# One bank for each head of a maxima piece, filled and read in turns, in the third causal attention of a decoder kernel

## What is computed

```python
H = 16; HD = D // H; NR = 64
c_q = einsum('bhtd,ld->bhtl', xh, W_DQ)
q_c = einsum('bhtl,dl->bhtd', c_q, W_UQ)
q_c_norm = _rms_norm(q_c, q_norm_w)
q_r = einsum('bhtd,rd->bhtr', q_c_norm, W_QR)
q = concatenate([q_c_norm, q_r]);  k = concatenate([k_c_norm, k_r])
scores = einsum('bhqd,bhkd->bhqk', q, k) * scale
causal = triu(full((t, t), -inf), k=1)
attn = softmax(scores + causal, axis=-1)
ctx = einsum('bhqk,bhkd->bhqd', attn, v_c)
out = einsum('bhtd,od->bhto', ctx, W_O)
```

## Time and profile before

| what | us |
|---|---|
| median of three runs | 3476.15 (3475.05 to 3477.63) |
| the profiled execution's own time | 3473.25 |
| its span in the profile | 3471.5 |
| TensorE matmul busy | 3022.5 (87%) |
| VectorE busy | 1858.8 (54%) |
| ScalarE busy | 1336.8 (39%) |
| GpSimd busy | 1138.8 (33%) |
| reductions L3621 (192), busy / idle ahead of them | 182.3 / 107.6 |
| maxima matmuls L3511 (384), busy / idle ahead of them | 92.2 / 46.8 |
| first and last reduction L3621 start at | 2952.0, 3269.2 |

### The profile page before, as it was taken

One profiled execution on the slowest core, in us unless ns is written; L12 is line 12 of the kernel. 1 busy time (PEld: TensorE's weight loads), 2 busy tenths in 40 slices (PEclk: granted clock), 3 DMA queues, 4 the chain that ended last, 5 costly groups with the idle time before them and its releaser, 6 DMA issues. The chain is left out here.

```text
span 3471.5 us, 46986 instructions
## 1 busy us (share of the span) xinstructions
PE 3022.5 (87%) x17490; PEld 1943.4 (56%) x17490; DVE 1858.8 (54%) x3038; ACT 1336.8 (39%) x2244; POOL 1138.8 (33%) x995
## 2 busy tenths in 40 slices
PE   7779999999999979999987876999685767888877
PEld 6645555555555448888855564666463555333345
DVE  6655666566566653233258743111448848666575
ACT  3324444444444443333331633332332425354543
POOL 0126566566666630000034312332242303111232
PEclk9889999999999989999998978999897889799989
DMA  1100000000000002101101034221201000000000
GB/s 55 52 1 1 1 1 1 1 1 1 1 1 1 1 27 61 55 27 59 31 17 34 1 124 141 34 34 23 45 1 33 1 16 2 1 1 1 1 28 28
DMA packets 108642, 81.89 MB, mean 24 GB/s; under 512 B 22283, under 2 KB 102182, under 8 KB 108422
## 3 DMA queue, kind: packets, MB, share of 16 engines
q1 hardware_dynamic: 94693, 65.15, 6.1%
q0 software_dynamic: 7488, 9.48, 1.7%
q10 hardware_dynamic: 6240, 4.26, 0.4%
HBM read 68.31 MB, written 11.47 MB: 23 GB/s over the span
## 5 line engine op out<-in xcount | busy, mean ns | idle before, releaser
L778 POOL TENSOR_TENSOR acc<-acc,pf 128x512 f32<-128x512 f32 (+1 forms) x448 | 564.0, 1281 | 254.7 <-ACT pf L905 254.7
L962 DVE TENSOR_REDUCE mxa<-ps 128x1 f32<-128x512 f32 x512 | 327.0, 680 | 229.3 <-PE ps L824 227.4
L905 ACT ACTIVATE pf<-ps 128x512 f32<-128x512 f32 x512 | 277.9, 595 | 318.8 <-PE ps L799 293.4
L812 PE MATMUL ps<-pf,v 128*64 128x512 f32 (+1 forms) x1152 | 311.6, 619 | 0.0
L3621 DVE TENSOR_REDUCE mx<-ps 128x2 f32<-128x1024 f32 (+1 forms) x192 | 182.3, 957 | 107.6 <-PE ps L3515 84.5
L3609 ACT ACTIVATE pT<-ps 128x1024 f32<-128x1024 f32 (+1 forms) x192 | 153.0, 811 | 154.3 <-PE ps L3527 153.9
L1772 POOL TENSOR_TENSOR e<-e,sm 128x1232 f32<-128x1232 f32 x48 | 107.9, 2247 | 226.4 <-DVE sm L2027 226.4
L824 PE MATMUL ps<-kH,qH 64*128 64x512 f32 x512 | 158.2, 441 | 23.7 <-DVE mc L970 18.5
L1159 POOL TENSOR_TENSOR x<-x,ys 128x256 f32<-128x256 f32 x16 | 11.8, 739 | 508.9 <-DVE ys L1364 508.9
L2480 DVE TENSOR_SCALAR ys<-ps,xs 128x256 f32<-128x256 f32 x39 | 18.9, 484 | 251.4 <-PE ps L2299 251.4
L1830 PE MATMUL ps<-ident,e 128*77 128x128 f32 x768 | 123.3, 312 | 26.2 <-ACT pT L1937 25.1
(11 more groups left out here) (551 smaller groups left out, 7039.4 us busy)
## 6 DMA issues: line engine op xcount, KB each, us to landing
w_raw<-in_c_h SPq DMA_DIRECT2D x32, 512.0 KB, 4.1
w1a<-in_f_w SPq DMA_DIRECT2D x8, 1024.0 KB, 13.9
w2a<-in_f_w SPq DMA_DIRECT2D x8, 1024.0 KB, 13.0
w_raw<-in_c_w SPq DMA_DIRECT2D x32, 128.0 KB, 2.3
x<-in_x SPq DMA_DIRECT2D x1, 2048.0 KB, 8.5
moe_rows<-rowbuf ACTq DMA_DIRECT2D x4, 512.0 KB, 10.3
moe_acc<-x ACTq DMA_DIRECT2D x1, 2048.0 KB, 13.4
x<-moe_acc SPq DMA_DIRECT2D x1, 2048.0 KB, 8.1
```

The costliest lines, as they stand in the source:

```text
L778: pool.tensor_tensor(now[0:r, :], now[0:r, :], pf[0:r, n % RING, a, :], ALU.add).then_inc(added.sem, 1)
L812: ins = pe.matmul(g.bk(3)[SIDE[a], :], v[0:r, u // 2 % 2, t, u % 2 * P + a * HD:u % 2 * P + (a + 1) * HD], pf[0:r, n % RING, a, :], start= ...
L905: act.activation(pf[0:r, n % RING, a, :], g.bk(bk.bank[f"s{n}_{a}"])[0:r, :], ACT.Exp, bias=bias)\
L962: dve.tensor_reduce(mxa[:, q % 2, half, a, j:j + 1], g.bk(4 + a), AXX, ALU.max).then_inc(bk.release(f"m{q}_{i}_{a}"), 1)
```

## The change

For the pieces beside score tiles (from the second iteration on) a fill is now one head in one bank: head 0 in bank 4, head 1 in bank 5. TensorE's order in a slot becomes: scores of pair 0, first piece head 0, scores of pair 1, first piece head 1, second piece head 0, values, second piece head 1, transposes or projection. Each head has its own masking matmul behind it. VectorE reduces head by head, in the order of the fills. The 24 early pieces keep their form and their banks.

```diff
-        pair = lambda it, m: (4, 0, 2)[m % 3] if (it, m) in early else 4
-        fills += [(f"m{it}_{m}", pair(it, m)) for it, m in early + [p for n in every for p in maxima_in(*n)]]
+
+        pair = lambda m: (4, 0, 2)[m % 3]
+        fills += [(f"m{it}_{m}", pair(m)) for it, m in early]
+        fills += [(f"m{it}_{m}_{a}", 4 + a) for n in every for it, m in maxima_in(*n) for a in range(2)]
...
-                def maxima(it, m):
+                def maxima(it, m, parts=(0, 1)):
...
-                    pe.wait_ge(*bk.free(f"m{it}_{m}", 0))
-                    wide, b0 = max(wd, 2 * P), pair(it, m)
-                    for a in range(2):
+                    whole = len(parts) == 2
+                    name = f"m{it}_{m}" if whole else f"m{it}_{m}_{parts[0]}"
+                    pe.wait_ge(*bk.free(name, 0))
+                    wide, b0 = max(wd, 2 * P), pair(m) if whole else 4
+                    for a in parts:
...
-                        for a in range(2):
+                        for a in parts:
...
                     for p in beside[:1]:
-                        maxima(*p)
+                        maxima(*p, (0,))
                     if n + 1 < len(every):
                         scores(n + 1, 1)
+                    for p in beside[:1]:
+                        maxima(*p, (1,))
+                    for p in beside[1:]:
+                        maxima(*p, (0,))
                     values(n)
                     for p in beside[1:]:
-                        maxima(*p)
+                        maxima(*p, (1,))
...
+                    if whole:
+                        dve.tensor_reduce(mx[:, i, half, 2 * pr:2 * pr + 2], g.ps[:, pair(m):pair(m) + 2, 0:wd], AXX, ALU.max).then_inc(bk.release(name), 1)
+                    else:
+                        dve.tensor_reduce(mx[:, i, half, 2 * pr + a:2 * pr + a + 1], g.bk(4 + a)[:, 0:wd], AXX, ALU.max).then_inc(bk.release(name), 1)
...
                     for p in beside:
-                        maxima(*p)
+                        for a in range(2):
+                            maxima(*p, (a,))
```

More of the change, by code:

```diff
@@ L3513, in maxima @@
                     if diagonal:
-                        for a in range(2):
+                        for a in parts:
                             ins = pe.matmul(g.bk(b0 + a)[:, wd - P:wd], ident_b[:], ngq[:], start=False, stop=True, skip_group_check=True)
-                    ins.then_inc(bk.fill(f"m{it}_{m}"), 1)
+                    ins.then_inc(bk.fill(name), 1)
                 def scores(n, pr):
@@ L3616, in _, with maxima @@
             def _(dve):
-                def maxima(it, m):
+                def maxima(it, m, parts=(0, 1)):
                     i, half, pr = PIECES[m]
                     wd = min(CH, (i + 1) * P - half * CH)
-                    dve.wait_ge(*bk.full(f"m{it}_{m}", 0))
-                    dve.tensor_reduce(mx[:, i, half, 2 * pr:2 * pr + 2], g.ps[:, pair(it, m):pair(it, m) + 2, 0:wd], AXX, ALU.max).then_inc(bk.release(f"m{it}_{m}"), 1)
+                    whole, a = len(parts) == 2, parts[0]
+                    name = f"m{it}_{m}" if whole else f"m{it}_{m}_{a}"
+                    dve.wait_ge(*bk.full(name, 0))
+                    if whole:
+                        dve.tensor_reduce(mx[:, i, half, 2 * pr:2 * pr + 2], g.ps[:, pair(m):pair(m) + 2, 0:wd], AXX, ALU.max).then_inc(bk.release(name), 1)
+                    else:
+                        dve.tensor_reduce(mx[:, i, half, 2 * pr + a:2 * pr + a + 1], g.bk(4 + a)[:, 0:wd], AXX, ALU.max).then_inc(bk.release(name), 1)
                 def negated(it, cc):
                     last = HALF - 1 if cc == 0 else NP - 1
-                    dve.wait_ge(*bk.read(f"m{it}_{last}", 0))
+                    if it:
+                        for a in range(2):
+                            dve.wait_ge(*bk.read(f"m{it}_{last}_{a}", 0))
+                    else:
+                        dve.wait_ge(*bk.read(f"m{it}_{last}", 0))
                     src = mx[:, 0:TC, 0, :]
```

## The result

| | before | with the change |
|---|---|---|
| median of the runs | 3476.15 us | 3509.99 us |
| lowest to highest, 5 runs each | 3473.64 to 3477.63 | 3507.64 to 3512.22 |
| ratio, 95% interval | | 1.0098 (1.0086 to 1.0110) |
| span of the profiled execution | 3471.5 us | 3508.4 us |
| its mean granted clock | 0.932 | 0.924 |

What follows compares the result with a forecast made beforehand. TensorE's maxima loads were taken as held by VectorE's reductions (112.9 us of waits) over one shared bank pair. Slots +11.0, first iteration -0.3, clock -0.4 made +10.3 us: 3486.5 us on the median, range 3475 to 3494.

Steps and rivals of the forecast that it cites:

- One slot, walked: Timing of the attention stage's twelve slots: 3.32 us against 3.64 without other work; together +1.57 us an iteration.
- The lone head at a pair's full price: On TensorE, a head run without its partner costs all of a pair's further 0.23 us, not half.
- the reductions 0.61 apart: On VectorE, one-head reductions at 512 keys follow each other every 0.61 us, overlapping, rather than waiting for the pipe to empty.
- the values in the bank loop: On TensorE, the values matmuls, 1.00 us at 512 queries, lose a reduction's cover and lie inside the bank loop.
- the last part: Signs to look for: slots of 3.3 and 3.9 to 4.0 us, iteration 42.2, VectorE idle 0.7, load waits under 112.9.
- The order on TensorE, which weighs most: Second piece's head 0 goes ahead of the values and head 1 behind them, so the values lose their cover.
- The clock term: First iteration, low clock from 2977 to 2995 us: some +1 us for added matmuls, at most 4.9 won back; set at -0.4.
- I set -0.4 for both: First iteration: -0.4 us for doubled matmul prices at 1.2 GHz and a possibly earlier 2.4 GHz together.
- rival A: First iteration: fewer TensorE gaps bring 2.4 GHz sooner; all 4.9 us gives 3482, no difference; chance 0.23 with smaller losses.
- The clock pays it back: The rival that an earlier 2.4 GHz in the first iteration cancels the loss, giving 3482 us; chance 0.23 with smaller losses.
- Rival B: On TensorE, a lone head is cheaper, 0.12 instead of 0.23 us: 23 us less in all, -12, 3464 us; chance 0.09.
- Rival C: In half the 56 diagonal slots, one more TensorE shape change is exposed: +6 us more, 3492; chance 0.10 with the like.

Runs made afterwards that it cites:

- e1: Kernel before with its pairs kept, second piece moved ahead of the values as in the change; 3490.01 us in one run, beside 3472.04 for the kernel before.
- e2: Changed kernel with heads split, but the values left ahead of both heads of the second piece; 3507.14 us in one run.
- e9: The changed kernel again, unaltered, on another chip beside the kernel before; four runs from 3485.57 to 3515.12 us, ratio 1.0072.
- e4: Kernel before with six spare ScalarE copies ahead of the stage; 3481.96 us in one run.
- e8: Kernel before with twelve spare ScalarE copies ahead of the stage; 3468.16 us in one run.
- e15: Kernel before with two spare VectorE reductions (1024 and 256 elements) in slot 5, TensorE's work untouched; 3531.62 us, ratio 1.0151.
- e16: Kernel before with one spare VectorE reduction of 1024 elements in slot 5, TensorE's work untouched; 3514.79 us, ratio 1.0097.
- e3: Changed kernel with six spare ScalarE copies ahead of the stage; 3569.78 us in one run.
- e7: Changed kernel with twelve spare ScalarE copies ahead of the stage; 3531.18 us in one run.
- e11: Kernel before with heads split in slots 4 to 7 only, values ahead of the second piece there; 3506.05 us, ratio 1.0091.
- e12: Kernel before with heads split in slots 4 to 7 only, values first there, plus six spare ScalarE copies ahead of the stage; 3507.80 us, ratio 1.0074.
- e5: Changed kernel with each lone head's matmul on all 128 rows, so maxima are of two heads' summed scores; 3487.37 us in one run.
- e10: Changed kernel with lone heads on all 128 rows, timed again on a chip with the change; median 3487.92 us, ratio 1.0038.
- e13: Kernel before with heads split in slots 4 to 7, values first, those heads on all 128 rows with summed-score maxima; 3512.84 us, ratio 1.0107.
- e14: Kernel before with heads split in slots 4 to 7, values first, all 128 rows, exact maxima by GpSimd zero padding; 3516.16 us, ratio 1.0084.
- hybrid: Kernel before with heads split in slots 4 to 7 only, values first there; 3506.05 us, or 3507.80 with six spare copies ahead of the stage.

## Why the prediction was right and wrong

**The structure held.** "One slot, walked" gave twelve slot lengths, and all are right to 0.03 us. The lone head at a pair's full price, the reductions 0.61 apart and the values in the bank loop are all seen. That a lone head costs a pair's time was a choice of one bound of two, and it came true; of this price hung 23 us. Of what the last part named, slots of 3.3 and 3.9 to 4.0 us, an iteration of 42.2, 0.7 us idle ahead of the fourth reduction and fewer waits of the loads, everything came. "The order on TensorE, which weighs most" holds by e1 and e2: +2.5 us an iteration for the order alone with pairs, and -0.1 for the split alone with the old order.

**The clock term failed.** The forecast said "I set -0.4 for both", and rival A was "The clock pays it back". This is the step that failed: it read the clock as a price of the first 18 us only the earlier trace rows and asked how much of it could be won, and it put the clock behind these 18 us at nothing. In fact this stage can fall back to 1.2 GHz in its middle and stay there for tens of us: +18.5 us net in iterations 3 and 6, and +8.7 behind the last reduction. The kernel before showed two such falls, of 3.4 us, and the forecast neither read them nor asked what they would cost were they longer. That could be bounded from the earlier trace rows and the slots: 18 us there for 13.1 us of work, so by this estimate a stretch of 27 us costs about 7 to 8 (it was 10.2 in the changed kernel), and one in each of six iterations some 45. The case "the clock falls more often or for longer", with +5 to +45 us, was missing, and with it the upper part of the range. A small slip stands beside it: with all of the clock's help the sum is 11.0 - 0.3 + 1 - 4.9, nearly +7, and not +6.

**Rival B** (a lone head cheaper than 0.18 us) is out: a lone head takes 0.42 us as a first one, like a pair. **Rival C** (one more change of shape exposed in the diagonal slots) is out: they came in within 0.03 of their forecast. **Rival A** is out: the granted clock from 2977 to 2995 us is somewhat higher in the first profile, 0.62 against 0.51,

```profile
2977.00:2995.00 18.00, 17.01 (x76) 7.77 (x76) 8.36 (x15) 6.13 (x9) 3.26 (x8) 0.62 0.00 1
```

but with the doubled prices in it the first iteration is 0.8 us longer all the same. That fewer gaps brought the higher clock isn't shown. The same kernel in e9's profile has none of it:

```profile
2977.00:2995.00 18.00, 17.46 (x68) 7.86 (x68) 7.39 (x13) 4.88 (x8) 3.26 (x8) 0.50 0.00 1
```

There the first stretch at 1.2 GHz lasts until 3005.9 and the first iteration takes 51.1 us instead of 45.76. The kernel before varies there too: with copies ahead of the stage it is back at 2.4 GHz from 2984.0 (e4) and 2982.7 (e8) on, without them from 2994.6. So the somewhat higher clock of the first profile can be chance.

**What stays open.** Shown is that the falls make most of the loss, and that they come without lone heads (e15, e16). The stretch at the start of the stage changes from one execution of a kernel to the next (e9) and between versions that differ only ahead of the stage (e3, e7). The later falls keep to their places: slot 0 of iterations 3 and 6 in the change, e9 and e7, the same slots in e11 and e12, slot 9 in e15; e3 alone of the change's versions has them elsewhere. Shown is also that full rows in all slots keep the clock up (e5, e10), and that full rows in four slots don't (e13, e14).

What decides whether a fall comes and how long it lasts isn't settled. One reading was only argued: the falls mostly begin in the diagonal slots, 8 to 1, and it may be worst where the length of the iteration brings the same slots round each time that the clock is about to fall, as in e15. Two things speak against length alone. e2 has an iteration of 40.53 us, that of the kernel before, and falls for 27.3 us in iterations 2, 4 and 6; and of three kernels at 42.1 us one never falls. Nor are these the slots in which TensorE is least busy by its records: before, at 2.4 GHz, it is busy all the time in slots 2 and 9 and for two thirds of the time in slots 4 and 7, where neither this kernel nor the change nor e15 has a fall begin.

No version beat the kernel before. The hybrid has the shortest iteration, 39.48 us, and would save some 8 us at before's clock, an estimate from seven iterations; nothing was found that keeps the clock up for it.

## What to carry to other kernels

Walk a slot from the starts of weight loads and reductions: it gave the new length of this loop to 0.1 us before it ran, and it shows that an operation which a wait now stands in front of has lost its cover. Then read the granted clock of the whole loop of before, not of its first us, and price every slot at 1.2 GHz too: a loop that touches the lower level for a few us may stay there for tens once it is changed, whichever way its structure goes, as e2 and the hybrid do here with a loop no longer than before. Before a gain or a loss of under 1% is put down to an edit, time a kernel with TensorE's work untouched and the loop as long as the edit makes it (e15 here), and compare executions at the same mean clock, of which there must be several for each version.

## What the hardware showed that was not expected

- The same loop body has two lengths, 42.13 us at 2.4 GHz and 67.59 at 1.2 (e3), and stays at the lower one for up to 198 us. In the 145 us of it shown above TensorE is busy for 98% of the time.
- Work on VectorE alone brings TensorE's clock down: an iteration that it makes 1.5 us longer at 2.4 GHz takes 10.7 us more in e15 (51.3 against 40.64).
- A lone head and the next scores' matmuls load at the same time when they use different halves of the rows. e2's weight loads in slot 4 begin 0.01 us apart:

```profile
3041.13 0.18 PEld L3529 LDWEIGHTS ps<-kT,qT 64*128 64x128 f32 x1 [0.76 <-DVE mx L3644]
3041.14 0.29 PEld L3545 LDWEIGHTS ps<-qT,kT 64*128 64x128 f32 x2
```

  Its slots 4 and 7 take 2.93 us and not the expected 3.38, which fits. With full rows (e13) slot 4 takes 3.57.
